# One recurrent step's matrix product in four column tiles, and units planned to end before the step

## What is computed

```
def step(h, z_t):
    gate = sigmoid(h @ Wh.T + z_t @ Wz.T + b)
    h_new = tanh(h * (1 - alpha) + gate * z_t)
```

## Time and profile before

| | us |
|---|---|
| median of 3 runs | 439.76 (439.58 to 440.62) |
| the profiled execution | 439.82 |
| its span, first to last instruction | 437.8 |
| first to last load of a step's weights | 43.0 to 338.7 |
| PE busy | 414.9 |
| DVE busy | 291.6 |
| ACT busy | 249.4 |
| POOL busy | 86.2 |

### The profile page before, as it was taken

One profiled execution on the slowest core, in us unless ns is written; L12 is line 12 of the kernel. 1 busy time (PEld: TensorE's weight loads), 2 busy tenths in 40 slices (PEclk: granted clock), 3 DMA queues, 4 the chain that ended last, 5 costly groups with the idle time before them and its releaser, 6 DMA issues.

```text
span 437.8 us, 13080 instructions
## 1 busy us (share of the span) xinstructions
PE 414.9 (95%) x4568; PEld 306.4 (70%) x4568; DVE 291.6 (67%) x983; ACT 249.4 (57%) x869; POOL 86.2 (20%) x366
## 2 busy tenths in 40 slices
PE   2999999899999999999999999899999999999994
PEld 2777877767777778777566767657765776777772
DVE  5875665877566665666458766447753987996662
ACT  3642664554663664654755447575657555756881
POOL 6320321231231331222322123121111000000000
PEclk9999999999999999999999999999999999999998
DMA  8510000000000000000000000000000100100001
GB/s 299 199 20 9 5 1 1 1 2 1 1 2 1 1 2 2 1 1 1 2 1 0 2 3 3 0 2 4 2 2 3 26 3 6 24 4 4 10 23 25
DMA packets 11222, 7.70 MB, mean 18 GB/s; under 512 B 8983, under 2 KB 10263, under 8 KB 11159
## 3 DMA queue, kind: packets, MB, share of 16 engines
q1 hardware_dynamic: 10727, 6.61, 4.9%
q10 hardware_dynamic: 432, 0.27, 0.2%
HBM read 5.39 MB, written 1.05 MB: 15 GB/s over the span
## 4 chain that ended last, share of the span: by engine, by line
PE 80%; ACT 9%; DVE 7%; issue 2%; DMA 1%; POOL 1%; DVEq 0%; ACTq 0%
PE ybk L1068 18%; PE cbk L1242 12%; PE hid L1221 10%; PE ybk L1193 6%; PE vbk L1221 4%; DVE cbk L1568 3%; PE hid L1119 3%; PE cbk L1246 2%; PE hid L1094 2%; ACT hb L916 2%; PE hid L1169 2%; ACT dd L990 2%; PE hid L1053 2%; PE cbk L1169 2%; ACT hs L995 1%
## 5 line engine op out<-in xcount | busy, mean ns | idle before, releaser
L1568 DVE TENSOR_TENSOR_SCAN cbk<-dd 128x24 f32<-128x24 f32 x256 | 55.6, 217 | 100.3 <-ACT dd L990 96.8
L1242 PEld LDWEIGHTS cbk<-hs,rec 128*128 128x128 f32 x512 | 76.3, 188 | 55.8 <-ACT hs L995 47.3
L1068 PE MATMUL ybk<-hg,down 128*128 128x256 f32 x352 | 100.3, 400 | 0.8 <-DVE hg L1447 0.5
L806 POOL TENSOR_TENSOR dd<-hs,leak 128x8 f32<-128x8 f32 x256 | 55.7, 218 | 229.2 <-ACT hs L995 225.5
L1242 PE MATMUL cbk<-hs,rec 128*128 128x8 f32 x512 | 92.5, 253 | 4.7 <-ACT hs L995 1.8
L995 ACT ACTIVATE hs<-cbk 128x8 f32<-128x8 f32 x256 | 45.3, 177 | 65.6 <-DVE cbk L1568 64.4
L990 ACT ACTIVATE dd<-cbk 128x8 f32<-128x8 f32 x256 | 46.4, 181 | 55.6 <-PE cbk L1242 54.6
L1221 PE MATMUL hid<-xsp,up 128*128 128x256 f16 x486 | 70.9, 277 | 0.4 <-DVE lg L1386 0.3
L1068 PEld LDWEIGHTS ybk<-hg,down 128*128 128x128 f32 x352 | 58.7, 191 | 6.3 <-DVE hg L1447 1.6
L1221 PEld LDWEIGHTS hid<-xsp,up 128*128 128x128 f16 x486 | 46.7, 106 | 8.7 <-issue 0.7
L1447 DVE TENSOR_TENSOR hg<-hb,hid 128x512 f32<-128x512 f32 x50 | 33.5, 676 | 2.6 <-PE hid L1053 2.5
(11 more groups left out here) (235 smaller groups left out, 658.2 us busy)
## 6 DMA issues: line engine op xcount, KB each, us to landing
qz<-up_in SPq DMA_DIRECT2D x3, 512.0 KB, 7.4
out_dram<-silu SPq DMA_DIRECT2D x4, 256.0 KB, 3.1
x<-x_in SPq DMA_DIRECT2D x7, 128.0 KB, 9.4
down<-down_in SPq DMA_DIRECT2D x1, 768.0 KB, 9.6
att<-att_in SPq DMA_DIRECT2D x1, 743.0 KB, 10.7
down<-down_in SPq DMA_DIRECT2D x1, 640.0 KB, 6.1
kp<-mrow SPq DMA_DIRECT2D x32, 4.0 KB
qz<-rows SPq DMA_DIRECT2D x32, 2.0 KB, 1.7
```

The lines of the kernel that those rows point to most:

```text
L806: tts(dd[:, t % ZR, 1, :, 2], hs[:, t, :], leak[:, 0:1].broadcast_to([P, B]), ALU.mult).then_inc(decay, 1)
L1068: m = pe.matmul(ybk[l][:, 0:n], D(l, "w2" if shared else "e2", e * f + i), hg[:, hg_of[made] % NHG, i * n:i * n + n], start=first and i == ...
L1242: pe.matmul(cbk[c % 2][:, o:o + B], wh, hs[:, t, :], start=False, stop=True, skip_group_check=True).then_inc(gate_pre, 1)
L1568: nc.vector.tensor_tensor_scan(vps[chunk_of(t) % 2], dd[:, t % ZR, 0].rearrange("p b o -> p (b o)"), dd[:, t % ZR, 1].rearrange("p b o -> ...
```

## The change

A step's product is written as four products, each with 32 columns of `wh` and the matching 32 output partitions; the semaphore that the gate waits for is incremented by the last. And PE's SLACK goes from .1 to 0.0, so that a unit may no longer be planned to end up to 0.1 us after the next step is expected. The planner's cost and shape of a step are left as they were.

```diff
--- before.py
+++ after.py
@@ -67,7 +67,7 @@
 
 ACT_LAST = ("E", "S", "K", "Q", "GT")
 ENGINES = ("pe", "act", "dve", "pool")
-SLACK = {"pe": .1, "act": .05, "dve": .05, "pool": .1}
+SLACK = {"pe": 0.0, "act": .05, "dve": .05, "pool": .1}
 WINDOW = {"pe": .88, "act": .45, "dve": .88, "pool": .88}
 
 
@@ -1239,8 +1239,10 @@
                     o = (t - STARTS[c]) * B
                     if t:
                         pe.wait_ge(h_full, t)
-                    pe.matmul(cbk[c % 2][:, o:o + B], wh, hs[:, t, :], start=False, stop=True,
-                              skip_group_check=True).then_inc(gate_pre, 1)
+                    for j in range(P // HP):
+                        m = pe.matmul(cbk[c % 2][HP * j:HP * j + HP, o:o + B], wh[:, HP * j:HP * j + HP], hs[:, t, :], start=False,
+                                      stop=True, skip_group_check=True)
+                    m.then_inc(gate_pre, 1)
                     for i in range(repeats.get(t, 0)):
 
                         pe.matmul(cbk[(c + 1) % 2][:, 256:512], id16[:], same, start=False, stop=True,
```

## The result

The changed kernel takes 444.10 us (median of 4 runs, 443.61 to 444.34) against 440.16 before (4 runs, 439.58 to 440.62): ratio 1.0089, interval 1.0071 to 1.0106. It is slower by 0.9%, 3.9 us. The forecast was 442.4, 2.6 above the 439.8 that it started from.

A forecast was written before the change was run, and what follows sets the result against it. The steps' chain sets the pace, with PE close behind. Intervals 289.8, plus 7.5 of waits and 1 for unequal intervals, give 298.3, 2.6 more; 439.8 + 2.6 = 442.4 us, eight in ten 433 to 455.

The forecast's parts named there:

- The step's product: Each recurrence step: four tiled products end at 0.25 us, not 0.39; gate starts at 0.32 rather than 0.42.
- light interval: Step-to-step interval with PE's other matmuls under 0.72 us, mostly 0.65; 86 forecast at 1.02 us each.
- The switch: Between steps and neighbouring matmuls: changing tile shape costs 0.09 us of PE time; loads start 0.07 before the matmul's end.
- The rival by which it hardly costs: Tile-shape changes in the recurrence cost half of 0.09 or nothing, giving 435 or 427 us; chance 0.25.
- The new account of PE: Recurrence interval: larger of 1.01 and PE's other matmuls plus 0.28 (f16 next) or 0.38 (fp32 next); sum 289.8 us.
- The full heaps: Recurrence intervals with 0.86 to 0.87 us of other PE work: 53 at 1.158 (f16 next), 72 at 1.242 (fp32 next).
- The 7.5 us of waits for other engines: Recurrence before the change: count gives 288.2 us, trace 295.7; the 7.5 difference is kept in the forecast.
- the 1 us set aside for unequal intervals: Recurrence: 1 us added because the order is planned for equal intervals of about 1.12 but meets 1.02 next to 1.24.
- The rival by which light intervals stay at 1.12: The 86 intervals with least PE filling don't get shorter: +8.6, giving 451 us; chance 0.15 for 447 to 455.
- The 99 us behind the steps have no step in them and keep their work: Attention stretch after the recurrence: stays at 99 us, adding nothing to the forecast.
- By itself the edit is worth about nothing: SLACK 0.0 without tiles gains about nothing; with tiles, the old order's count would be 292 to 293.
- PE's waits for the state much below 49 us: Sign that the forecast is right: PE's waits for the new state in the recurrence fall much below 49 us.

The follow-up runs named there:

- The pair of added products: Kernel before plus one unread f16 product of 8 columns behind each step: 32 weight columns 464.60 against 439.69 us; 128 weight columns 440.55, ratio 1.0020.
- SLACK alone: Kernel before with PE's SLACK at 0.0 and the step left as one product of 128 columns: 443.33 against 440.57 us, ratio 1.0061.
- two tiles: Changed kernel with every step as two products of 64 columns in two column tiles: 451.91 us against 439.69 before, ratio 1.0295.
- the kernel with 151 tiled steps: Changed kernel with only the 151 steps next to full intervals tiled, the others one product of 128 columns: 451.19 us against 440.57 before, ratio 1.0230.

## Why the prediction was right, and where not

- *The step's product.* Loads 0.16, end 0.25, gate 0.32: all three as worked out from L1193's and L1242's rows. The chain of a light interval is 1.02, as forecast.
- *The switch*, 0.09 of PE time, at 0.07 before the end: confirmed. In the 70 steps that PE holds back behind an f16 matmul of 256 columns, the first load starts 0.201 behind that matmul's start, where the array was free after 0.108, so 0.093; behind an fp32 pass, in 61 steps, it is 0.307 - 0.216 = 0.091. The pair of added products shows it as a cause. The rival by which it hardly costs fell. (The profile's ends of matmuls are modelled, and so is the 0.07; the spacings of starts don't hang on it.)
- *The new account of PE.* The full heaps came where they were put: 1.158 (53; 71 at 1.162, which part of the others joined) and 1.242 (72; 79 at 1.241). At 1.02 there are 66 where 86 were forecast, and 21 at 1.09. The 7.5 us of waits for other engines, kept from before without a reason, came out as 7.2 (296.95 - 289.8). The recurrence grew by 1.4, not 2.6: the 1 us set aside for unequal intervals was not needed.
- *The rival by which light intervals stay at 1.12* fell: no interval is left there. The 21 at 1.09 aren't its work in the main: 8 of them are middle ones of 0.80, so that 0.80 + 0.28 = 1.08 is PE's time, and 7 hold 32 passes of L1193.
- *"The 99 us behind the steps have no step in them and keep their work"* is the step that failed, a term put at nothing. They have no step, but the planner left them more: the order shows it (8 products of L1102 and 3 of L1094 more), and I counted only up to the last step. It cost 2.6 us, two thirds of the measured difference: 1.6 of work, 0.7 in a gap whose cause is not shown, 0.3 by the clock. The work is the edit's. The gap stands at the same place in three kernels of this order (this one, SLACK alone, two tiles), and the clock varies from execution to execution.
- *"By itself the edit is worth about nothing"* failed for the same reason: the interval count was right (0.3 us), the end was not looked at (+3.2). With the tiles the count was right too: 292 to 293 in the old order against 289.8, and 3.2 us measured.
- *"PE's waits for the state much below 49 us"* was wrong as a sign: they rose to 71, since a drain shows as idle time released by the state. Without the 28 us of drains they are 46.5, down from 54, so not "much" lower either.
- So the forecast of +2.6 against +3.9 is one term too high by 1.2 and one missing of 2.6. That they have opposite signs, and bring the number close, is luck; what the prediction had right is the mechanism within the recurrence.

## What to carry to other kernels

Putting narrow tiles among full-width matmuls of 256 columns cost TensorE 0.09 us of its time for the drain ahead of each tiled step, so narrow tiles pay in a latency chain only where the engine would wait anyway: count its filling for each interval and tile by that, not everywhere. When a planner's number changes, count what it leaves behind the stretch as well as in it. And read "waits for the state" on an engine whose shape changes against the time at which the state was there.

## What was not expected of the hardware

Among 128-column work a product of 32 weight columns costs 24.9 us and one of 128 columns in its place 0.9, 256 of each: 0.094 us more for one, which has two drains in it. That is a mean over light intervals, which take them up, and full ones, which pay for both.

The increment by the last of four column tiles reaches ScalarE 0.066 us behind the end that the trace gives (0.316 - 0.250), against 0.046 for the last of two tiles of 64 columns (0.336 - 0.290) and 0.036 for one product of full width. The ends are modelled, so part of this may lie in the model.

TensorE's granted clock falls to its lower level, 1.2 GHz, at the end of each profiled execution, when PE's work comes in pieces with pauses of 0.5 to 0.8 us between them, and the last product is run at either level or half and half: 1.10, 1.38, 1.89, 2.00 and 2.04 us in five kernels. In the clock row of the changed kernel's page (tenths of full speed) only the last of 40 slices shows it:

```profile
PEclk9999999999999999999999999999999999999997
```

For the last product alone that is up to 0.9 us of a kernel's time, and differences of that size in the stretch behind the steps should not be read as the edit's. Pauses aren't the only occasion. Twice the clock fell amid dense work and came back: for 6.9 us in the kernel with 151 tiled steps (0.51 from 346.5 on; PE was busy for 6.06 of the 6.50 us ahead), and for 3.4 us in the one with the tiled product behind each step:

```profile
76.00:81.60 5.60, 5.60 (x47) 5.15 (x45) 3.39 (x13) 2.72 (x12) 0.85 (x4) 1.00 0.00 0
81.60:85.00 3.40, 3.40 (x14) 2.72 (x14) 1.69 (x11) 1.00 (x5) 0.41 (x2) 0.50 0.00 0
```

What sets that off, no run here shows.
